# Embedding gathers in a factorization-machine kernel: each waits for the third one ahead of it, and transposes stand eight units apart

## The reference

```python
e = jnp.stack([tbl_0[ids[:, 0]], ..., tbl_39[ids[:, 39]]], axis=1)
p = e[:, rowidx]
q = e[:, colidx]
z = jnp.einsum('bie,fie,bif->bi', p, param, q)
h = jnp.concatenate([z, dense_ctx], axis=1)
h = jnp.maximum(h @ W_top1 + b_top1, 0.0)
h = jnp.maximum(h @ W_top2 + b_top2, 0.0)
y = h @ W_top3
```

## Time and profile before

| | before |
|---|---|
| median of three runs | 1416.8 us |
| the profiled execution | 1417.29 us |
| its span, first to last instruction | 1415.5 us |
| PE busy | 1317.9 us (93%) |
| DVE busy | 931.2 us (66%) |
| POOL busy | 605.8 us (43%) |
| ACT busy | 84.8 us (6%) |
| mean granted TensorE clock | 0.981 of full speed |
| mean busy share of the DMA engines, slices 4 to 40 of 40 | between 0 and 2 tenths |

### The profile page before, as it was taken

How to read it: one execution, slowest core, us unless ns; L and a number is a source line. 1 busy time by engine, 2 the same in 40 slices (tenths; PEclk the granted TensorE clock), 3 DMA queues, 4 the chain that set the end, 5 groups by cost and what they waited for, 6 DMA issues and landing times.

```text
span 1415.5 us, 16721 instructions
## 1 busy us (share of the span) xinstructions
PE 1317.9 (93%) x7024; PEld 465.6 (33%) x7024; DVE 931.2 (66%) x803; ACT 84.8 (6%) x137; POOL 605.8 (43%) x646
## 2 busy tenths in 40 slices
PE   0468999999989999999999999999999999999999
PEld 0123333333333333333333333333333333333333
DVE  0245777777765457777875567788786556888870
ACT  0000000000000000000000000000000000000001
POOL 4555555555455555554555555545555540000000
PEclk9679999999999999999999999999999999999999
DMA  4111222222222122222222222222222111111100
GB/s 135 26 41 52 61 63 57 64 57 62 63 50 49 48 56 63 64 64 62 63 65 49 49 50 63 62 62 64 64 65 57 46 47 45 45 52 45 52 2 1
DMA packets 50498, 77.35 MB, mean 55 GB/s; under 512 B 14004, under 2 KB 14260, under 8 KB 50296
## 3 DMA queue, kind: packets, MB, share of 16 engines
q1 hardware_dynamic: 29936, 55.26, 13.0%
q0 software_dynamic: 20480, 21.01, 7.7%
q10 hardware_dynamic: 8, 0.01, 0.0%
HBM read 76.22 MB, written 0.01 MB: 54 GB/s over the span
## 4 chain that ended last, share of the span: by engine, by line
PE 70%; POOL 12%; DMA 11%; issue 7%; DVE 0%; ACT 0%; POOLq 0%
PE ring L316 38%; PE z_ps L329 20%; POOL stage L185 12%; DMA stage<-tbl,idx 11%; PE aux L265 6%; PE aux L290 2%; PE aux L272 2%; PE ring L265 1%; PE ring L317 1%; PE ring L272 0%; PE aux L279 0%; DVE prod L255 0%; DMA idx<-ids_t 0%; PE ring L279 0%; POOLq L184 0%
## 5 line engine op out<-in xcount | busy, mean ns | idle before, releaser
L255 DVE TENSOR_TENSOR prod<-ring,emb 128x1024 f32<-128x1024 f32 x800 | 931.0, 1219 | 445.6 <-PE ring L317 342.1
L185 POOL DMA_INDIRECT stage<-tbl,idx x640 | 605.1, 945 | 556.0 <-DMA stage<-tbl,idx 396.6
L316 PE MATMUL ring<-emb,raw 64*128 64x512 f32 x1600 | 777.6, 619 | 7.2 <-issue 4.4
L317 PE MATMUL ring<-emb,raw 64*128 64x512 f32 x1600 | 777.7, 619 | 0.0
L316 PEld LDWEIGHTS ring<-emb,raw 64*128 64x128 f32 x1600 | 282.5, 190 | 443.5 <-issue 374.9
L329 PE MATMUL z_ps<-prod,sel 128*32 128x512 f32 x3200 | 384.8, 598 | 0.0
L317 PEld LDWEIGHTS ring<-emb,raw 64*128 64x128 f32 x1600 | 282.1, 190 | 0.0
L329 PEld LDWEIGHTS z_ps<-prod,sel 128*32 128x32 f32 x3200 | 83.4, 109 | 272.1 <-issue 178.2
L290 PE MATMUL aux<-ident,stage 128*128 128x128 f32 x320 | 55.1, 297 | 86.8 <-DMA stage<-tbl,idx 86.8
L197 ACT ACTIVATE emb<-aux 128x512 f32<-128x512 f32 x80 | 47.9, 599 | 781.6 <-PE aux L290 671.3
L290 PEld LDWEIGHTS aux<-ident,stage 128*128 128x128 f32 x320 | 35.5, 147 | 149.7 <-issue 148.2
(11 more groups left out here) (19 smaller groups left out, 14.8 us busy)
## 6 DMA issues: line engine op xcount, KB each, us to landing
raw<-param_b SPq DMA_DIRECT2D x200, 256.0 KB
stage<-tbl,idx POOLq DMA_INDIRECT x640
W<-W1g SPq DMA_DIRECT2D x1, 1792.0 KB
W<-W2t SPq DMA_DIRECT2D x1, 512.0 KB
idx<-ids_t SPq DMA_DIRECT2D x1, 240.0 KB, 4.4
z<-dense_t SPq DMA_DIRECT2D x4, 32.0 KB
idx<-ids_t SPq DMA_DIRECT2D x1, 80.0 KB, 1.9
out<-y_out ACTq DMA_DIRECT2D x4, 2.0 KB
```

What stands on the lines that cost most here:

```text
L185: pool.indirect_dma_start(stage[:, n % STAGE, t, E * (f % 2) : E * (f % 2) + E], None, tables[f], bass.IndirectOffsetOnAxis(ap=idx[:, c, f ...
L255: dve.tensor_tensor(prod[:, slot : slot + 2, :], ring[:, n % RING, :, :], by, ALU.mult).then_inc(prod_done, 1)
L316: pe.matmul(ring[:, n % RING, 0, :], w[0:E], emb[0:E, c % 2, m, :], start=True, stop=True)
L317: pe.matmul(ring[:, n % RING, 1, :], w[E:P], emb[E:P, c % 2, odd, :], start=True, stop=True).then_inc(unit_ready, 1)
```

## The change

The number of gathers in flight, `FLIGHT`, goes from 4 to 3, and its meaning changes. Gather number `made` (0 to 639) now signals `gathered[made % 3]` and, from the fourth gather on, waits on the same semaphore until all that signalled it before have landed, the latest of them being gather `made - 3`. The wait and the `sem_inc` now stand ahead of 637 gathers, where they stood ahead of 159. The semaphores are three, not six, and PE waits for all three, each with the count of the gathers up to the end of its duo. `TURN` goes from 9 to 8: from duo 9 on, duo n is transposed before unit 40 + 8 (n - 9), so duo 79 before unit 600. The first ten stay where they were.

```diff
-TURN = 9
-FLIGHT = 4
+TURN = 8
+FLIGHT = 3
...
-        gathered = [sem(f"gathered{i}") for i in range(STAGE)]
+        gathered = [sem(f"gathered{i}") for i in range(FLIGHT)]
...
-                    if i % FLIGHT == 0 and (n or i):
-                        at = n if i else n - 1
-                        pool.wait_ge(gathered[at % STAGE], 16 * (2 * BT * (at // STAGE) + (i or 2 * BT)))
+                    made = 2 * BT * n + i
+                    if made >= FLIGHT:
+                        pool.wait_ge(gathered[made % FLIGHT], 16 * (made // FLIGHT))
                         pool.sem_inc(pool_waited, 1)
                     pool.indirect_dma_start(
                         stage[:, n % STAGE, t, E * (f % 2) : E * (f % 2) + E], None, tables[f],
                         bass.IndirectOffsetOnAxis(ap=idx[:, c, f, t : t + 1], axis=0),
-                    ).then_inc(gathered[n % STAGE], 16)
+                    ).then_inc(gathered[made % FLIGHT], 16)
...
-                    pe.wait_ge(gathered[at % STAGE], 16 * 2 * BT * (at // STAGE + 1))
+                    for j in range(FLIGHT):
+                        pe.wait_ge(gathered[j], 16 * -((j - 2 * BT * (at + 1)) // FLIGHT))
```

## The result

| | before | changed |
|---|---|---|
| median of four runs of each | 1416.17 us | 1508.88 us |
| lowest and highest | 1413.8, 1416.88 | 1507.39, 1514.16 |
| span of the profiled execution | 1415.5 us | 1507.4 us |
| PE busy | 1317.9 us | 1335.6 us |
| mean granted TensorE clock | 0.981 | 0.96 |

The ratio is 1.0664, with a 95% interval of 1.0635 to 1.0693. The forecast was 1359 us. On which chip these runs were made isn't on record. So both numbers need an explanation.

A forecast was written before the change was run, and what follows sets the result against it. Gathers were taken to bound the kernel to 421.6 us, PE after that. An earlier end of PE's waiting (-53.9 us) and cheaper transposes (-3.4) took the span from 1415.5 to 1358.2, median 1359 us; range 1345 to 1385.

The forecast's parts named there:

- The pace of the gathers: POOL's gathers start 1.25 us apart, 10.0 us a duo where it was 14.0; duo 0 lands at 19.0 us.
- The waits behind the third one ahead: Each gather's wait for gather n - 3 is over 0.53 us before it can hold POOL, so costs nothing.
- rivals A and B: A: landings slow with three in flight, 1.5 us a gather, 1380 us, chance 0.14. Rival B has its own line.
- The sum for an undisturbed chip: Whole kernel: 1415.5 us less 53.9 and 3.4 gives 1358.2 of span, a median of 1359; chance 0.78.
- the transposes' places: PE-bound part: 38 of 51 remaining duos move from inside a batch (0.80 us) to its edge (0.71): -3.4 us.
- PE is the bound from there to the end: Behind duo 7 (92.5 us), eight units and a duo cost PE 11.7 us, above POOL's 10.0; PE sets the pace.
- Rival C: DVE holds up the descriptors of POOL's gathers: pace over 2 us a gather, time above 1500 us, chance 0.01.
- Rival B: POOL's dispatch isn't hidden: 1.72 us a gather, gathers the bound to the end, about 1455 us, chance 0.06.

The follow-up runs named there:

- `noinc`: `turn9` without the increment of the unused semaphore behind each gather's wait; 1357.87 us on chip 6, 0.9599 of the kernel before.
- `turn9`: The changed kernel with the transposes nine units apart again (`TURN` 9, not 8); 1358.89 us on chip 1, 1499.93 us on chip 13.

## Why the prediction was wrong

- **The pace of the gathers: right.** 1.25 us each; duo 0 at 19.76 us (19.0 forecast), duo 3 at 49.66 (49.0). The waits behind the third one ahead never held POOL in the row, and rivals A and B fell with that.
- **The sum for an undisturbed chip: right within 11 us.** 1347.93 was measured against 1359. The term that was too small is that of the transposes' places. Away from the layers, duos at a batch's edge all cost 0.60 us (11.56 less two batches of 5.48), not 0.71 on average. From unit 211 to the end the undisturbed profile is 10.9 us shorter than the one before (981.9 against 992.8), where 3.4 were forecast; unit 211 itself came at 363.4, where 367.7 was. On chip 6 the two distances differ by 10 us (1347.93 against 1357.87 for `noinc`, which leaves out the increment too; `turn9` took 1358.89 on chip 1). The late products that I had averaged in the earlier trace rows, 679.60 to 686.25, fit the pattern of held-back increments and aren't a property of the edge; that wasn't tested by itself.
- **"PE is the bound from there to the end": this step failed.** It took for granted that what PE finishes is known to the others at once, at whatever pace POOL issues gathers. On some chips it isn't, and this cost 162 us in the profiled execution. The kernel before had rows of four gathers and hardly a late product, and no rival asked whether a row of seventy does to the other engines what four didn't.
- **The side of the outcome came from none of the rivals.** Rival C was nearest, gathers that disturb other engines, but by descriptors that starve. The gathers' own durations stayed at 939 to 1100 ns, median 947, as in the earlier trace rows, so nothing like it shows: the gathers keep their pace and the rest waits. The rule of the Trainium skill that the prediction named ("SBUF — State Buffer", section "SBUF: two separate sides") is about operations of DVE in a two-port mode. The prediction took the product for one without a reason, and no run shows that it is, so the trace doesn't test the rule.
- **Rival B's arithmetic: right, in other kernels.** A chain slower than 1.66 us a gather makes the program gather-bound at a distance of eight: 1489 at 1.76, 1510 at 1.80. The same distance that wins 10 us with fast gathers loses 96 with the old ones (1510.4 against 1414.44).

## What to carry to other kernels

A throttle that pauses may do more than limit what is in flight. Before a pause is taken out of a chain, ask what else drains in it, and try a thinner even pace beside the densest one: here, at the distance of nine, 1.55 us a gather gains 3.0% on chip 13, where 1.25 loses 6.1%; on chips that hold nothing back 1.25 gains 3.9 to 4.0%.

When a comparison of two files contradicts the order of their instructions, as `turn9` did, repeat both in one job on one chip. The view that shows the trouble is the list of waits: idle time that "remote" ended, on a kernel of one core, in pieces of microseconds. Time that "issue" ended is no sign by itself.

## What the runs showed of the hardware that was not expected

- Chips differ, for a kernel on one core. On chip 13 rows of gathers at 1.25 us hold PE's increments back (in all 8 such kernels); on chips 1 and 6 they don't (in 6). The kernel before runs alike on all (1414.1 to 1416.7 us). Chip 13 showed it in three jobs, but chips 1 and 6 were seen in one job each, so that it is the chip and not something else about a job rests on chip 13. What differs is open.
- In the long row increments come 11.2 us apart, and so in every profile with that row on chip 13, but for one or two steps of 9.8 to 10.5 us in each. After POOL's last gather of the row (107.12 us) the next still came at 114.84 and 119.22. What sets the 11.2 us, and which part of the chip holds the increments back, wasn't found.
- Increments by DVE and ACT and the landings of DMAs arrived in time in the same stretch (83.17 to 83.31 us, 71.35 to 71.44, and gathers every 1.25 us).
- Two gathers of POOL leave 0.30 us between them in which a memset of 0.11 us costs nothing.
- Nothing in these runs hung, and spacing the gathers ended the trouble. The Trainium skill ("VectorE: DVE Perf Modes", section "The TRN2 errata — SBUF-src ops pay a fixed extra latency per instruction") warns that semaphore increments at a high rate from one engine can deadlock another, and says to space them. It speaks of a deadlock, not of lateness; whether the two have one cause no run here tells.
